# New slot tables and bank hold times for a fused attention and LayerNorm kernel

## What is computed

```python
xn = layernorm(x)                                   # over 512 columns
q = (layernorm(xn) * norm_g + norm_b) @ Wq          # 16 heads of 64
k, v = split(xn @ Wkv)
k, v = concat(null_k, k), concat(null_v, v)         # 2 null columns
q, k = l2norm(q) * q_scale, l2norm(k) * k_scale
sim = (q @ k.T) * 8 - slope[h] * |j - i|            # ALiBi, causal mask
attn = softmax(sim) @ v
out = x + attn @ Wout + ffn(xn)
```

## Time and profile before

| | us |
|---|---|
| median of 3 runs | 3038.81 |
| lowest and highest run | 3033.42, 3042.46 |
| span of the profiled execution | 3041.3 |
| PE busy in it | 2821.4 |
| DVE busy | 2666.3 |
| POOL busy | 2330.5 |
| ACT busy | 2117.3 |

### The profile page before, as it was taken

The page is one execution under the profiler, slowest core; times in us unless marked ns, Lnnn a source line. Parts: engine busy times, 40 slices in busy tenths (PEclk is TensorE's granted clock), DMA queues, the critical chain, the costliest instruction groups (busy, mean ns, idle before and its releaser), DMA issues. The chain is left out here.

```text
span 3041.3 us, 84128 instructions
## 1 busy us (share of the span) xinstructions
PE 2821.4 (93%) x31759; PEld 1647.2 (54%) x31759; DVE 2666.3 (88%) x6386; ACT 2117.3 (70%) x3380; POOL 2330.5 (77%) x2588
## 2 busy tenths in 40 slices
PE   3589999999999999999999999999999999999998
PEld 3245555555555555555555555555555555555554
DVE  6678989889999899898998899988998988989886
ACT  2467767776776767777777777777677776676775
POOL 5886687976789677886869768797678966788663
PEclk8799999999999999999999999999999999999999
DMA  4111232312332133222333123231233213332121
GB/s 148 44 27 35 58 71 60 70 31 67 72 73 50 31 76 67 72 42 43 77 62 78 35 56 74 61 72 31 67 72 70 54 31 67 77 67 47 33 35 42
DMA packets 457537, 178.17 MB, mean 59 GB/s; under 512 B 421552, under 2 KB 423600, under 8 KB 457136
## 3 DMA queue, kind: packets, MB, share of 16 engines
q1 hardware_dynamic: 455664, 172.69, 26.1%
q10 hardware_dynamic: 1472, 0.09, 0.0%
HBM read 55.23 MB, written 16.78 MB: 24 GB/s over the span
## 5 line engine op out<-in xcount | busy, mean ns | idle before, releaser
L1022 DVE CUSTOM_DVE_ANT_0 PS<-PS,STR 128x512 f32<-128x512 f32 (+3 forms) x1536 | 822.3, 576 | 118.3 <-PE PS L1262 116.5
L563 ACT ACTIVATE AR<-PS,SC 128x1024 f32<-128x1024 f32 (+1 forms) x640 | 658.3, 1029 | 325.5 <-PE PS L1270 152.3
L1214 PE MATMUL PS<-WH,XT 128*128 128x388 f16 x2048 | 678.1, 331 | 88.0 <-DVE AR L1029 77.8
L1217 PE MATMUL PS<-WL,XT 128*128 128x388 f16 x2048 | 678.4, 331 | 0.0
L1218 PE MATMUL PS<-WH,XT 128*128 128x388 f16 x2048 | 677.7, 331 | 0.0
L789 POOL TENSOR_TENSOR RN<-SS,HALF 128x8 f32<-128x8 f32 x256 | 428.6, 1674 | 302.6 <-DVE SS L1104 295.5
L567 ACT ACTIVATE AR<-AR 128x1024 f16<-128x1024 f32 (+1 forms) x640 | 621.8, 972 | 20.4 <-ACT AR L563 0.2
L1056 DVE TENSOR_TENSOR AR<-AR 128x768 f16<-128x768 f32 (+1 forms) x448 | 593.9, 1329 | 15.6 <-ACT AR L567 14.7
L1239 PE MATMUL PS<-AR 64*128 64x512 f16 (+3 forms) x4608 | 498.6, 325 | 4.7 <-ACT AR L563 4.5
L1287 PE MATMUL PS<-AR 128*128 128x66 f16 x4608 | 474.9, 193 | 10.6 <-POOL AR L772 10.5
L1289 PE MATMUL PS<-AR 128*128 128x64 f16 x4608 | 474.5, 194 | 0.0
(11 more groups left out here) (241 smaller groups left out, 5613.0 us busy)
## 6 DMA issues: line engine op xcount, KB each, us to landing
XW<-in_L_attn_x SPq DMA_DIRECT2D x112, 256.0 KB, 2.8
out<-ACC SPq DMA_DIRECT2D x64, 256.0 KB, 2.1
ACC<-in_L_attn_x SPq DMA_DIRECT2D x56, 256.0 KB, 2.9
AR<-QKB SPq DMA_TRANSPOSE x512, 2.5
AR<-in_L_attn_Wkv SPq DMA_DIRECT2D x2, 1536.0 KB, 13.8
ACC<-in_L_attn_x SPq DMA_DIRECT2D x2, 1024.0 KB, 7.4
AR<-in_L_attn_Wout SPq DMA_DIRECT2D x1, 2048.0 KB, 9.1
AR<-CTK SPq DMA_TRANSPOSE x128, 2.4
```

The lines of the kernel that those rows point to most:

```text
L563: e.activation(PR[:, n % 2, :, 0:wide], SB[:, :, 0:wide], ACT.Exp, scale=SIG).then_inc(s_p, 1)
L1022: e.tensor_tensor_reduce(out=r[:, 0:n], in0=r[:, 0:n], in1=ST[:, u % 2, h, o:o + n], scale=1.0, scalar=LOW, op0=ALU.add, op1=ALU.max, accu ...
L1214: e.matmul(PJ, XT[:, k, xs], WH[:, k, p, :], start=k == 0, stop=False)
L1217: e.matmul(PJ, XT[:, k, xs], WL[:, k, p, :], start=False, stop=False)
```

## The change

Nearly all tables and the five values of `HOLD` get other numbers. Instructions, operands, waits and the number of instances stay the same; what changes is the order in which each engine's queue holds them, and which bank (and so whose reader) a piece, `op`, `ntp` or `otp` waits for. Two examples: in the new tables the `vl` of tile 6 stands in slot 43 with `ss` of group 2 behind it, where `ss` stood in slot 39 and `vl` in slot 42; the eight statistics, once 4 slots apart, are spread over slots -217 to -73.

```diff
--- before.py
+++ after.py
@@ -47,51 +47,51 @@
 STEPS = [(qc, [(kt, 0)]) if kt < 4 * qc + 2 else (qc, [(kt, 0), (kt + 1, 256)]) for qc in range(2) for kt in range(4 * qc + 3)]
 NS = len(STEPS)
 PL_POOL = (0, 4, 7)
-W_PIECE = [45, 46, 48, 57, 64, 66, 70, 74, 77, 82, 84, 91]
-W_MAX = [46, 49, 52, 57, 63, 64, 69, 74, 82, 82, 84, 91]
-W_SCORE = [91, 94, 100, 105, 108, 114, 118, 122, 126, 132]
-W_PLOW = [97, 100, 101, 108, 115, 116, 122, 128, 133, 135]
-W_VALUE = [100, 105, 105, 115, 120, 127, 136, 136, 139, 140]
-W_ON = [108, 144]
-W_OTP = [112, 151]
-W_OTS = [109, 150]
-W_OTL = [111, 151]
-W_OP = [117, 120, 139, 142, 153, 154, 163, 170]
-W_ADD = [115, 121, 141, 146, 158, 158, 163, 177]
-W_PROJ = [z for z in [-1, 7, 12, 23, 28, 32, 40, 43] for k in range(KC)]
-W_KV = [2, 7, 13, 23, 29, 34, 41, 44]
-W_VL = [3, 10, 15, 23, 27, 35, 42, 46]
-W_STRIP = [29, 42]
-W_SQ = [10, 27, 42, 48]
-W_SS = [13, 23, 39, 49]
-W_POW = [18, 30, 47, 53]
-W_TP = [36, 45, 56, 69]
-W_HI = [24, 35, 52, 58]
-W_LO = [27, 39, 56, 65]
-W_ROWS = [50, 94]
-W_SHIFT = [69, 91]
-W_CTP = [75, 99]
-W_NX = [73, 95]
-W_NL = [76, 102]
-W_NTP = [87, 108]
-W_NT = [87, 108]
-
-W_XA = [-98, -94, -90, -86, -82, -78, -74, -70]
-W_STAT = [-94, -90, -86, -82, -78, -74, -70, -66]
-W_XB = [-60, -49, -37, -36, -23, -13, -11, 8]
-W_XF = [-49, -47, -32, -28, -13, 1, 12, 21]
-W_XH = [-44, -41, -28, -15, -12, 4, 14, 22]
-W_XL = [-36, -36, -26, -8, -5, 9, 29, 34]
-W_XTP = [-33, -30, -22, 4, 10, 20, 22, 41]
-W_SMALL = [-63, -60, -58, -57, -53]
-W_VSC = [-27]
-W_BASE = [74, 85, 98, 103, 107, 125, 136, 152]
-W_BN = [80, 85, 102, 113, 119, 132, 151, 167]
-W_BM = [88, 93, 101, 114, 123, 140, 158, 177]
-W_BA = [88, 97, 108, 122, 137, 145, 165, 184]
-
-
-HOLD = [4.6, 5.2, 7.1, -60.5, 5.5]
+W_PIECE = [45, 46, 54, 58, 61, 65, 67, 72, 79, 84, 87, 91]
+W_MAX = [46, 51, 54, 60, 64, 67, 70, 76, 84, 85, 88, 93]
+W_SCORE = [91, 94, 103, 106, 108, 113, 116, 121, 128, 133]
+W_PLOW = [98, 104, 104, 110, 118, 119, 124, 130, 136, 138]
+W_VALUE = [103, 106, 106, 112, 118, 128, 137, 139, 139, 147]
+W_ON = [108, 147]
+W_OTP = [110, 151]
+W_OTS = [110, 153]
+W_OTL = [112, 153]
+W_OP = [113, 125, 139, 148, 154, 154, 162, 172]
+W_ADD = [117, 128, 141, 148, 156, 157, 165, 178]
+W_PROJ = [z for z in [5, 9, 13, 21, 30, 34, 42, 43] for k in range(KC)]
+W_KV = [5, 10, 15, 21, 31, 37, 40, 45]
+W_VL = [8, 10, 19, 25, 31, 38, 43, 49]
+W_STRIP = [39, 43]
+W_SQ = [12, 27, 41, 49]
+W_SS = [12, 26, 43, 52]
+W_POW = [19, 33, 48, 58]
+W_TP = [36, 43, 57, 67]
+W_HI = [21, 37, 54, 59]
+W_LO = [28, 39, 56, 62]
+W_ROWS = [66, 93]
+W_SHIFT = [70, 93]
+W_CTP = [83, 93]
+W_NX = [71, 99]
+W_NL = [79, 108]
+W_NTP = [90, 109]
+W_NT = [86, 107]
+
+W_XA = [-254, -210, -202, -142, -108, -99, -91, -69]
+W_STAT = [-217, -202, -166, -106, -102, -82, -79, -73]
+W_XB = [-72, -31, -23, -12, -10, -4, 10, 34]
+W_XF = [-49, -26, -14, -9, 1, 9, 26, 33]
+W_XH = [-49, -26, -11, -4, 0, 10, 29, 34]
+W_XL = [-46, -18, -4, 6, 13, 18, 33, 38]
+W_XTP = [-36, -8, -5, -3, 11, 25, 38, 38]
+W_SMALL = [-64, -62, -61, -59, -53]
+W_VSC = [-2]
+W_BASE = [67, 86, 99, 109, 111, 118, 144, 153]
+W_BN = [78, 88, 102, 110, 118, 137, 151, 168]
+W_BM = [83, 92, 106, 116, 123, 139, 161, 174]
+W_BA = [84, 105, 111, 120, 134, 153, 166, 182]
+
+
+HOLD = [5.6, 5.9, 6.1, -85.9, 6.5]
 
 LATE_ACT = [0, 1, 5, 6, 9, 10, 15, 16, 18, 24, 25, 27, 32, 33, 38, 39]
 LATE_DVE = [1, 2, 6, 7, 10, 11, 16, 17, 19, 25, 26, 28, 33, 34, 39, 40]
```

## The result

The changed kernel takes 2937.0 us (median of 4 runs, 2935.2 to 2943.6), the kernel before 3040.6 on the same chip: ratio 0.9676, 95% interval 0.9658 to 0.9694. The profiled execution has a span of 2941.8 us against 3041.3, 99.5 less. The prediction had said 2990, with 2955 as the lower end.

A forecast was written before the change was run, and what follows sets the result against it. PE's matmuls are the floor, so only its 220 us idle could be won. Per batch 8.0 us won less 1.5 of new stalls is 6.5, over 7.74 batches 50 us: 3041.3 to 2991, stated as 2990, range 2955 to 3042.

The forecast's parts named there:

- piece 10: PE stall of 0.18 us per unit waiting for piece 9's bank; triangle matmuls placed between remove 1.4 us per batch.
- PE's 346.13 per batch stays: PE's busy time, 346.13 of 360.84 us per batch, was taken as unchanged because no instruction is added.
- the surplus of lo and pl: Extra DVE time of lo and pl from contention with POOL, 98 us for lo alone; taken as unchanged.
- the caps of the crowded windows: Third window (POOL nearly full) gains only 0.5 of 3.45 us idle, fourth (DVE nearly full) 0.6 of 2.62.
- The last two: Seventh and eighth windows of the batch, where DVE carries statistics and normalising: 4.9 of 5.62 us idle won.
- the four others: The four windows of the batch not shown, with DVE less busy: 2.0 of 3.02 us idle won.
- ntp 1: New small stalls on PE: 0.6 us per batch from nl moved on POOL, 4 x 0.2 for its bank.
- Piece 6: Takes piece 5's banks after 1.3 us instead of 3.1; costed at nothing while DVE is on time.
- Slower by overlaps: Rival: surplus of lo and pl grows in the four crowded windows; 3048 to 3090 us, chance 0.12.
- each stall comes back one stage on: Rival: nothing moves, DVE and POOL set the period everywhere; within 9 us of now, chance 0.10.
- the second: Rival: new bank waits, ntp 1 at 1.0 and piece 6 at 0.4 us per unit; 3010 to 3030, chance 0.14.
- the fourth: Rival: LayerNorm moved ahead frees POOL, two crowded windows give 4 of 6.07 us; 2960 (2940 to 2972), chance 0.12.

The follow-up runs named there:

- ss 2 alone in the kernel before: Kernel before with one number changed: sum of squares of group 2 in slot 42 instead of 39, behind vl of tile 6 on DVE; ratio 0.9996.
- The doubled lo: Changed kernel with lo of groups 0 and 3 done twice at the same places, order unchanged; ratio 0.9818, 43 us against after.

## Why the prediction was right and wrong

*What was right.* The direction, and the places. Over the span the shown waits fell from 40.9 to 1.9 us at projection 7, from 13.6 to 1.2 at piece 5, from 11.9 to 0.8 at piece 10, from 6.8 to nothing at op 1 and from 13.3 to 7.0 at piece 8, of which 6.3 stand in unit 0. ss waits behind vl, and 0.46 us came back at piece 1 of unit 30 where 0.5 was put down. The start got 3.3 us longer, within the 5 it was given, and the drain 3.6 shorter where nothing was forecast. Net idle time per batch was to fall by 6.5 us and fell by 7.6; this part of the sum alone, 7.74 batches, is 50 us forecast and 63.8 measured in the whole middle.

*What was wrong first: "PE's 346.13 per batch stays".* It fell by 3.95, 31 us over 7.74 batches and 35.4 in the whole middle. The step took busy time for work. Waits too short to be shown hide in it, 27 us less of them over six batches by the sum of steps above. (The price of changing between 64 and 128 rows hides in it too, but it is the same in both kernels.) The short waits are at the same doors as the long ones, so opening them gives back more than the trace calls idle: piece 10 was priced at 1.4 us per batch and gave 2.7. The prediction had no rival for this term, and so its range had no room for it. Of the 49.5 us by which the span fell beyond the forecast 50, 35.4 are this term and 13.5 are idle time of PE in the middle; start and drain nearly cancel.

*Second: the surplus of lo and pl, "taken the same as now".* The text named it (98 us for lo) and bounded it both ways, but then let only the upward side make a rival, and called the downward side "hardly on PE's path". lo lost 64 us and pl 76. The doubled lo shows that added DVE work reaches the time by about a half, so it is not "hardly on PE's path"; how much of the 99 us the saved work gave is not shown. The reason given for "no change", mostly the same neighbours, failed too: what pow and its followers stand beside changed for groups 0 and 3.

*Third: the caps of the crowded windows.* The third was given 0.5 and gave 1.16, since POOL's busy time there fell from 45.17 to 42.26 and the stall on pl in it went. The fourth was given 0.6 because DVE would stand at 45.5 of 46.12; it stands at 41.37 with two statistics more and gave 0.94. The last two gave 6.47 instead of 4.9, the four others 2.98 instead of 2.0. These are lengths: the new stalls are already taken off and the hidden time is in them, 11.55 us in all against a net 6.5 forecast.

*New stalls.* ntp 1 was to cost 1.4 us per batch (0.6 for nl and 0.2 in four units for the bank). It costs 3.0 in the batch shown, 19.0 over the span in 14 places: right in cause, nl behind sq and add 5 behind ss 0, short by half in size, and rarer and longer than put. Piece 6 cost next to nothing, as forecast (3.4 us over the span, in two places at its start); nothing new came up at the transposes.

*The rivals.* Slower by overlaps had the right mechanism with the wrong sign. The rival "each stall comes back one stage on" is true of ss 2 alone in the kernel before. No other single move into that kernel won anything either (HOLD nothing, the statistics a loss of 7 us, lo of 32), and it is false of all moves together. Two sums among the rivals do not come out: for 0.4 us at piece 6 in each of 62 units the second should add 25 us and not 12, and by its own terms (4.9, 2.0 and 4, less 1.5) the fourth comes to 9.4 us per batch, 73 us and about 2966, not 10.5, 81 and 2960. The fastest rival, 2960, named the third and fourth windows; most of the extra came elsewhere, from the last two and from PE's busy time.

*What stays open.* How the 99 us divide: the 63.8 idle and 35.4 busy are read off, but how much of either is owed to DVE's 140 us less work, and how much to queues that fit better, was not separated. The LayerNorm tables alone (but for the statistics), pieces and max alone, and the orders of POOL and ACT alone were not run.

## What to carry to other kernels

When only an order changes, PE's busy time is not a constant: compare the steps between starts in a stalled and an unstalled unit, and count the difference as idle time that can be won. Where engines run static queues that feed each other, one table moved alone tells little of the whole change: here it gave nothing or a loss, while all tables together gave 3.2%. Out of the changed kernel, one or two numbers moved back or on cost up to 77 us. Give the contention term the same weight in both directions, and price it by how much of the engine's added work comes through, here about a half.

## What the runs showed of the hardware

- A change between 64-row and 128-row matmuls costs about 0.1 us each way without being shown as idle: 0.26 instead of 0.16, and 0.31 instead of 0.22 from start to start.
- A DVE operation with two SBUF inputs stood still behind a 1024-column operation of POOL (1.83 us instead of 0.68) and was not held up beside POOL's power on 8 columns (0.69; 107 such cases with a mean of 0.03 us above the shortest).
- A wait of PE of up to about 0.2 us is not shown as idle: in the kernel before piece 10 started 0.40 us after a matmul that is otherwise followed after 0.055, with 0.18 in the bracket.
- In the two runs with the most stalls of PE the mean granted clock was 0.952 and 0.942 (DVE's tables alone, PE's tables alone) against 0.984 in the changed kernel. Between 200 and 2800 us it was 0.96 and 0.95 against 1.00. In either run some 220 of the 2048 steps from L1217 to L1218 are over 0.25 us, most of them 0.33 instead of 0.16; in the changed kernel 47 are. So a part of their loss is clock; how much was not worked out.
